# Values of the second attention in both row halves at once, the last FFN products in the S ring, later memsets, and a new order

## What is computed

```python
x = x + _L0_xattn_ref(_layernorm(x, axis=-1), ctx_512, ctx_512)
x = x + _L0_ffn_ref(_layernorm(x, axis=-1), w_router, w_fc, w_proj)
x = x + _L1_xattn_ref(_layernorm(x, axis=-1), ctx_512, Wq, Wkv_expand, Wout)
x = x + _L1_ffn_ref(_layernorm(x, axis=-1), down_w, ..., e7_b2)
```

## Time and profile before

| | us |
|---|---|
| median of 3 timed runs | 364.07 (361.49 to 364.35) |
| the profiled execution, whole | 360.21 |
| its span, first to last instruction | 358.4 |
| TensorE busy (3260 matmul records) | 329.3, 92% |
| VectorE busy | 218.9, 61% |
| ScalarE busy | 161.2, 45% |
| GpSimd busy | 105.6, 29% |

### The profile page before, as it was taken

How to read it: one execution, slowest core, us unless ns; L and a number is a source line. 1 busy time by engine, 2 the same in 40 slices (tenths; PEclk the granted TensorE clock), 3 DMA queues, 4 the chain that set the end, 5 groups by cost and what they waited for, 6 DMA issues and landing times.

```text
span 358.4 us, 8192 instructions
## 1 busy us (share of the span) xinstructions
PE 329.3 (92%) x3260; PEld 270.2 (75%) x3260; DVE 218.9 (61%) x566; ACT 161.2 (45%) x345; POOL 105.6 (29%) x190
## 2 busy tenths in 40 slices
PE   0977599999999899999999999899998999998896
PEld 0655477887887788778789688787886887886783
DVE  7789887988897415738257747327373566437235
ACT  1576742557433324441143721445524455445550
POOL 7795315342148512242252271123300000200000
PEclk9968869999999999999999999999999999999999
DMA  8999914336342300034500088300607000300300
GB/s 174 407 379 311 144 30 89 60 59 119 61 81 38 60 2 2 2 60 82 96 4 2 2 190 164 121 2 2 118 2 146 3 2 29 123 0 15 134 0 29
DMA packets 62997, 29.95 MB, mean 84 GB/s; under 512 B 58672, under 2 KB 61040, under 8 KB 61680
## 3 DMA queue, kind: packets, MB, share of 16 engines
q1 hardware_dynamic: 62960, 29.43, 34.1%
HBM read 14.71 MB, written 1.08 MB: 44 GB/s over the span
## 4 chain that ended last, share of the span: by engine, by line
PE 78%; DVE 15%; issue 2%; ACT 2%; DMA 1%; POOL 1%; DVEq 0%; POOLq 0%
PE Y L1352 26%; PE H L1352 23%; PE S L1352 19%; PE S L1397 4%; PE S L1421 2%; DVE MN L1124 2%; DVE PT L1125 2%; DMA QT_OT<-KQS 1%; PE S L1430 1%; PE S L1508 1%; DVE KS L1305 1%; DVE KQS L1184 1%; PE S L1360 1%; DVE K L1111 1%; DVE MN L1131 1%
## 5 line engine op out<-in xcount | busy, mean ns | idle before, releaser
L1352 PE MATMUL H<-XT,WF 128*128 128x256 f32 x256 | 62.7, 392 | 0.0
L1352 PE MATMUL Y<-WP,A 128*128 128x256 f32 x256 | 60.6, 383 | 0.0
L1005 POOL TENSOR_TENSOR A<-R 128x512 f32<-128x512 f32 x32 | 33.5, 1049 | 83.0 <-ACT R L861 79.2
L1352 PEld LDWEIGHTS H<-XT,WF 128*128 128x128 f32 x256 | 48.0, 195 | 6.6 <-issue 0.2
L1352 PEld LDWEIGHTS Y<-WP,A 128*128 128x128 f32 x256 | 47.0, 190 | 6.9 <-issue 0.9
L889 ACT ACTIVATE A<-H,B 128x256 f32<-128x256 f32 x84 | 35.5, 471 | 35.4 <-PE H L1352 35.2
L1352 PE MATMUL Y<-A,W 128*128 128x256 f32 x168 | 44.0, 386 | 0.4 <-DVE KS L1305 0.3
L1352 PE MATMUL H<-CD,W 128*128 128x256 f32 x168 | 42.3, 381 | 0.7 <-ACT CD L878 0.7
L861 ACT ACTIVATE R<-H 128x512 f32<-128x512 f32 x32 | 19.0, 597 | 43.5 <-PE H L1352 43.5
L1305 DVE SCALAR_TENSOR_TENSOR KS<-Y,Y0n,PT 128x256 f32<-128x256 f32 x32 | 15.5, 484 | 33.6 <-PE Y L1352 33.3
L1352 PEld LDWEIGHTS Y<-A,W 128*128 128x128 f32 x168 | 30.8, 190 | 6.5 <-ACT A L889 1.6
(11 more groups left out here) (185 smaller groups left out, 547.5 us busy)
## 6 DMA issues: line engine op xcount, KB each, us to landing
PT<-gates SPq DMA_DIRECT2D x4, 1024.0 KB, 5.4
W<-in_w SPq DMA_DIRECT2D x2, 1344.0 KB, 10.9
WF<-in_wf SPq DMA_DIRECT2D x2, 1024.0 KB, 7.4
WP<-in_wp SPq DMA_DIRECT2D x2, 1024.0 KB, 9.5
X<-in_x SPq DMA_DIRECT2D x8, 128.0 KB, 8.1
out_dram<-X SPq DMA_DIRECT2D x8, 128.0 KB, 1.7
CD<-in_ctx_in SPq DMA_DIRECT2D x2, 256.0 KB, 5.4
C<-in_ctx_in SPq DMA_DIRECT2D x1, 256.0 KB, 3.0
```

The costliest lines, as they stand in the source:

```text
L1005: nc.gpsimd.tensor_tensor(flat(A0[:, n % 2, :, :]), R0[:, n % 2, :], R0[:, n % 2, :], ALU.mult).then_inc(a0_ready, 1)
L1352: return nc.tensor.matmul(o, a, b, start=start, stop=stop, skip_group_check=shared)
```

## The change

Five things are edited. `values1` becomes one step for a tile: it claims two S banks and issues each head for the first and then for the second row half before it goes to the next head. `widen` becomes one step for a group: it claims two S banks instead of Y banks, issues the four GX products of both tiles, waits for `acc_ready`, and issues the two ACC products. `turn_back` and the planner's needs follow that. `setup` is called behind the queries of tile 3 (`BY_PE` is 3). And the planner has other numbers: a factor 1.6 on TensorE's costs in its first 28 us, other costs for the two merged steps, and a new `SWITCH`, `CHANGE`, `SLACK` and `URGENCY`. The instructions themselves are the same in number and shape but for the one order in which they stand.

```diff
-FILLS |= {..., ("ffn1", "y"): "Y", ("ffn1", "o"): "Y"}
+FILLS |= {..., ("ffn1", "y"): "Y", ("ffn1", "o"): "S"}
-SWITCH = 4675.9
-CHANGE = 50
-SLACK = {"act": 0.012, "dve": 0.508, "pe": 0.073, "pool": 0.8, "sp": 0.43}
+WARM, COLD = 28.0, 1.6
+SWITCH = 5849.7
+CHANGE = 389.7
+SLACK = {"act": 0.269, "dve": 0.663, "pe": 0.034, "pool": 0.02, "sp": 2.535}
 URGENCY = {
-    "const": "z 495.1 -1827.6  i -1698.9 11411.7  m -31438 30090  g 15446 18381.6  ",
+    "const": "z -8309.8 2028.3  i -37057.4 28289.9  m -42281.7 18451.7  g 20100.5 27985.8  ",
...
+            d *= COLD if at < WARM else 1.0
...
-                if t == 1:
+                if t == BY_PE:
                     setup()
...
-                    read_out(pe, part, t, "o", 0 if part == "attn0" else 1)
+                    for i in range(1 if part == "attn0" else 2):
+                        read_out(pe, part, t, "o", i)
...
-            def values1(t, bt):
-
-                b, done = claim(pe, "attn1", t, "o", bt)
-                if bt == 0:
-                    read_out(pe, "attn1", t, "p", 1)
-                rows = slice(bt * S, (bt + 1) * S)
+            def values1(t, i):
+
+                if i:
+                    return
+                halves = [claim(pe, "attn1", t, "o", bt) for bt in range(2)]
+                read_out(pe, "attn1", t, "p", 1)
                 for hq in range(4):
                     for h4 in range(4):
                         h = 4 * hq + h4
-                        ins = mm(b[32 * h4:32 * h4 + 32, hq * S:(hq + 1) * S], V1[rows, t % 2, h, :], PT1[rows, t % 2, h, :])
-                ins.then_inc(done, 1)
+                        for bt, (b, done) in enumerate(halves):
+                            rows = slice(bt * S, (bt + 1) * S)
+                            ins = mm(b[32 * h4:32 * h4 + 32, hq * S:(hq + 1) * S], V1[rows, t % 2, h, :], PT1[rows, t % 2, h, :])
+                            if h == NH1 - 1:
+                                ins.then_inc(done, 1)
...
-            def widen(g, k):
-                b, done = claim(pe, "ffn1", g, "o", k)
-                if k == 0:
-                    pe.wait_ge(gx_ready, g + 1)
-                for dc in range(DC):
-                    mm(b[:, 0:D], GX[:, dc, k * P:(k + 1) * P], CW[:, dc, :], start=(dc == 0), stop=False)
-                if k == 0:
-                    pe.wait_ge(acc_ready, g + 1)
-                mm(b[:, 0:D], ACC[:, k * P:(k + 1) * P], UW[:, :], start=False).then_inc(done, 1)
+            def widen(g, i):
+                if i:
+                    return
+                pe.wait_ge(gx_ready, g + 1)
+                banks = [claim(pe, "ffn1", g, "o", k) for k in range(2)]
+                for k, (b, _) in enumerate(banks):
+                    for dc in range(DC):
+                        mm(b[:, 0:D], GX[:, dc, k * P:(k + 1) * P], CW[:, dc, :], start=(dc == 0), stop=False)
+                pe.wait_ge(acc_ready, g + 1)
+                for k, (b, done) in enumerate(banks):
+                    mm(b[:, 0:D], ACC[:, k * P:(k + 1) * P], UW[:, :], start=False).then_inc(done, 1)
```

More of the change, by code:

```diff
@@ L58 @@
                                             ("ffn0", "x r"), ("ffn1", "x r g d z")) for s in names.split()}
-FILLS |= {("ffn0", "u"): "H", ("ffn0", "y"): "Y", ("ffn1", "c"): "H", ("ffn1", "y"): "Y", ("ffn1", "o"): "Y"}
+FILLS |= {("ffn0", "u"): "H", ("ffn0", "y"): "Y", ("ffn1", "c"): "H", ("ffn1", "y"): "Y", ("ffn1", "o"): "S"}
 def ring_of(s):
@@ L77 @@
                   x="pe .23 act .37", w="pe .87 dve 2.34", q="sp 2.2", s="pe .6 dve .69",
-                  m="dve .38 pe .1 act .25", p="pe .70 act .6", o="pe .5 act .37", n="pe .45 dve .71",
+                  m="dve .38 pe .1 act .25", p="pe .70 act .6", o="pe .6 act .37", n="pe .45 dve .71",
                   a="pe .23 act .37", r="pe .87 dve .42"),
@@ L83 @@
                  e="act .2 dve 1.5", t="act .2 dve 1.2", d="pe .87 act 1.13", g="pe .2 act .27", gd="sp .5", gb="sp .5", c="pe .86 act .94",
-                 w="pe .43", y="dve .86", o="pe 1.3 dve .42", st="sp .5", b="act .22", zp="pool 12.0", z="pe 1.8 dve .16")}
+                 w="pe .43", y="dve .86", o="pe 2.6 dve .42", st="sp .5", b="act .22", zp="pool 12.0", z="pe 1.8 dve .16")}
 COST = {part: {s: [(e, float(d)) for e, d in zip(text.split()[::2], text.split()[1::2])] for s, text in costs.items()}
@@ L123, in work_of @@
     parts = list(COST[s[0]][s[2]])
+    if (s[0], s[2], s[3]) == ("attn1", "o", 1):
+        parts = parts[1:]
+    if (s[0], s[2], s[3]) == ("ffn1", "o", 1):
+        parts = parts[1:]
     if s[0] == "ffn1" and s[2] == "c" and 2 * s[3] + 1 == NCH1:
@@ L138, in claims @@
         return [(part, n, "y", EXPERTS.index(e))] if c == 0 else []
+    if (part, stage) == ("attn1", "o"):
+        return stages(part, n, "o*2") if i == 0 else []
+    if (part, stage) == ("ffn1", "o"):
+        return stages(part, n, "o*2") if i == 0 else []
     return [s] if (part, stage) in FILLS and stage != "y" else []
@@ L203, in attn1 @@
             add(a("p", i), a("m"))
-            add(a("o", i), a("p", 1))
+            if i == 0:
+                add(a("o", i), a("p", 1))
+            else:
+                add(a("o", i))
+                need(a("o", i), a("o", 0), of=0)
         add(a("k"), a("kv"))
@@ L208, in attn1 @@
         add(a("m"), a("s", 1))
-        add(a("n"), a("o", 1))
+        add(a("n"), a("o", 0), a("o", 1))
         add(a("a"), a("n"))
@@ L271, in ffn1 @@
         for k in range(2):
-            add(f("o", k), f("y", E1))
+            if k == 0:
+                add(f("o", k), f("y", E1))
+            else:
+                add(f("o", k))
+                need(f("o", k), f("o", 0), of=0)
             add(f("st", k), f("o", k))
@@ L290, in steps_and_needs @@
         ffn1(g)
-    first, last = {"ffn0": ("u", 0), "ffn1": ("c", 0)}, {"ffn0": ("d", BLOCKS0 - 1), "ffn1": ("o", 1)}
+    first, last = {"ffn0": ("u", 0), "ffn1": ("c", 0)}, {"ffn0": ("d", BLOCKS0 - 1), "ffn1": ("o", 0)}
     for a, b in zip(BODIES, BODIES[1:]):
```

## The result

The changed kernel takes 364.24 us (median of 20 runs), the kernel before 363.44 us in as many runs beside it; the ratio is 1.0086 with a 95% interval of 1.0050 to 1.0121. So the change makes the kernel 0.9% slower, where 1.5% faster was forecast, within the band of 1%. (Most executions of before lie in two groups, one around 359 us and one from 363 to 368; the ratio leaves out those that are over 1.5% above the fastest of their kernel, so it need not agree with the medians.)

The account below looks back on a forecast made before the run. TensorE was taken as the bound from 60 us on, VectorE up to about 50 us. Savings of 3.0 + 1.0 - 0.2 + 0.7 + 0.9 = 5.4 us gave 354.8 profiled, plus 3.86 a median of 358.7 us; 8-in-10 range 353.5 to 366.5.

Parts of the forecast that it names:

- Values: Second attention's values on TensorE: alternating row halves overlap, a tile takes 0.48 instead of 0.86 us, 3.0 us saved.
- The first rival: Values of the second attention: row halves do not overlap, the 3.0 us stay away, 361.7 us; chance 0.12.
- the fourth: Values of the second attention: alternating records cost 26 ns each, 6.5 us lost instead of 3.0 gained, 368.2 us; chance 0.03.
- Start: VectorE's chain at the start: earlier key copy and half a transpose wait, less 0.2 us for later memsets, net 1.0 us saved.
- The 0.6 us for the key copy: VectorE at the start: the key copy comes near 17.1 instead of 17.70 us, 0.6 us earlier.
- The 0.6 us for half of the wait of 1.27 us: VectorE's wait for the third key transposes: a block of scores now stands behind them, half the wait goes, 0.6 us.
- Middle: TensorE's waits between 100 and 280 us: 1.8 us gained, 0.5 and 1.5 lost, net 0.2 us lost.
- the 1.5 us for new waits: Middle of the kernel: allowance of 1.5 us lost to unseen waits in the new order of 400 steps.
- The known waits: TensorE's three waits, 4.0 us together: 220 to 240 goes, 100 to 120 partly, 260 to 280 stays or grows.
- the second rival: New order gives its gain back in many small waits, up to 6 us lost in the middle, 362.7 us; chance 0.14.
- Last group and end: Last two groups: router's sum and gates 0.7 us earlier; last add near 354.9 instead of 355.84, 0.9 us saved.
- The third rival: VectorE falls behind around 100 us, second attention's first queries come late, TensorE loses 9.9 us, 368.6 us; chance 0.10.

Follow-up runs that it names:

- the run with the later gates: Changed kernel with TensorE's turn of group 0's gates behind two more first-FFN down blocks, ScalarE's fifth up-block read ahead of the gates' copy: 1.0040, median 361.20 us.
- the four waits filled: Changed kernel with GpSimd's root first, final additions first, group 0's gates later and an up block between tile 1's probabilities: 0.9946 to the kernel before, median 357.36 us.

## Why the prediction was wrong

**Values: mechanism right, size wrong.** The term was 0.86 to 0.48 us for a tile, 3.0 us. A tile alone took 0.92 us before and takes 0.79, so 8 x 0.13, about 1.1 us (by the group's busy time 1.5, 8.6 to 7.1). I took the strips for the limit and, as they are freed, half the time. The first 32 records bear that out with 0.24 us; then another limit, hidden before by the strips (28 ns per matmul), sets the pace, and the other 32 take 0.40. What that limit is stays open. The first rival (no overlap) and the fourth (26 ns for each record) are both refuted. What the Trainium skill states of eight independent tiles (TensorEngine Tiling (Array Packing), "Available Configurations") holds for those 32 records only; its floor of some 25 ns between starts (TensorE: Matmul & The Clock Gate, "Wait — 56ns, not 53.3ns?") is not seen, with 7 ns between them and 0.64 us for the 32 matmuls of a tile, 20 ns each.

**Start: two steps failed.** The 0.6 us for the key copy came (0.8). The 0.6 us for half of the wait of 1.27 us was read from a stretch of before at a granted clock of 0.74; at the full clock the wait is gone in the old order too, so at that clock it was not the change's to gain. (In the run with the later gates, whose clock was 0.50 and 0.73 from 20 to 28 us, the new order still waits 0.52 of it, so at the low clock the half was about right.) And I didn't ask what is late next: VectorE's lead of 2.8 us was lost at a root on GpSimd that stands behind a key transfer which nothing in the change makes earlier. I followed VectorE and TensorE through the new order and not GpSimd, though its list has the root behind that spread in both kernels. Instead of 1.0 us, 0.2 are gained at the norms of group 0 (42.95 for 43.13), and TensorE stands still 2.6 us more up to 60 us, while it is busy 2.6 us less there. Moving the root alone brought the first up block 2.96 us earlier.

**Middle: the step that failed is the 1.5 us for new waits.** The known waits went as said, the narrow product of group 1 waited 1.5 us (2 forecast). The new ones are for the most part not many small ones, as the second rival had it, but two: 2.4 us for the gates of group 0, and 1.0 us inside 128 probabilities in a row. For the gates I didn't ask what VectorE's new list has between the router's logits and its sum; eight steps stand there, so the sum comes 4.66 us behind the exponentials, and TensorE's list has nothing else in front of the gates to fill the time. In 60 to 300 us the standstill rose from 4.6 to 7.9 us, 3.3 more where 0.2 was forecast. With the values' gain of 1.1 instead of 3.0 us (1.9 less) and the start's 0.2 instead of 1.0 (0.8 less) that is 5.8 of the 8.2 us by which the span missed the sum, 2.8 longer instead of 5.4 shorter; the rest is not accounted for. The second rival's 362.7 us is the nearest to the result, and it was added up wrongly: 6 us lost instead of 0.2 would be 5.8 us more, 364.5.

**Slower clock: not among the terms.** I counted a wait at its own length. Seven profiles, two of them of the changed kernel, have the wait of 2.4 us for the gates unchanged. In six of them the clock falls behind it, and some 1.6 us more are lost; the first profile of the changed kernel is the seventh, so the wait alone doesn't decide it, and the 2.8 us of span between the first two profiles contain nothing of this. In the three runs in which that wait was filled, the clock stayed full there.

**Last group and end: right.** From the last chunk of group 2 to the gates of group 3 it was 7.9 us (324.81 to 332.71) and is 7.2 (329.07 to 336.27): 0.7 us. From the last chunk to the last addition it was 4.42 us (351.42 to 355.84) and is 3.56: 0.9 us.

**The third rival** (VectorE late at 100 us) did not come: TensorE is busy without a break from 80 to 120 us.

**The median.** I added 3.86 us because the median of three shown lay that far above the profiled execution. The changed kernel's median of 20 lies 1.2 us above its own profiled execution, so the addition came from the executions drawn. It brought the forecast (358.7) nearer to the measured median by luck: against the profiled execution alone the sum is wrong by 8 us (354.8 against 363.05).

**What the moves show together.** With the four waits filled, the new order and the edits are 6.9 us faster than the changed kernel. So the loss lay in these waits as a group. Of the single moves the gates' is the best borne out, by its steps, its ratio and its time.

What stays open: what each edit brings or costs in the old order beyond the two places named, how much of the time the root's wait on GpSimd costs, what paces the second half of a tile's values, and why the instructions come late in some executions and not in others.

## What to carry to other kernels

A reordering is to be followed on every engine that feeds the critical one, the quiet ones too: ask of each step that gets ready earlier what stands in front of it in the queues of the engines that it still needs. Two microseconds of wait on TensorE can cost more than two, as the clock may fall behind them (1.6 us more here, in six profiles of seven), so a list should have other ready work in front of each result that comes late. Where many short matmuls stand in a row, look for a standstill without a semaphore in it: one such of 1.0 us cost here about as much as the shorter values of all eight tiles saved.

## What the runs showed of the hardware beyond this

In the tiles' runs of values, short matmuls in other strips and row halves start 7 ns apart for 32 records (0.24 us), and the next 32 take 0.40 us. Within runs of short matmuls TensorE stood still for 0.4 to 1.4 us between two starts with no semaphore there, and went on 1.3 to 1.5 us after an instruction transfer of 16 KB had ended. Some of VectorE's smallest operations took over four times as long while GpSimd worked: `dlt` took 0.68 us at 211.07, beside GpSimd's tensor operations, and 0.16 us at 219.17, and in all profiles it is 0.67 to 0.68 beside them and 0.16 without. The reciprocal (0.17 us) and the reduction to ranks (0.29) in the same chain took the same time beside GpSimd as without it. Over the chain from `dlt` to the gates this makes 4.87 us where 3.87 were needed before, 1.0 of the 2.4 us for which TensorE waits.
